# Counting a graph's adjacency matrix with one-hot products: 25 blocks of 50 target nodes, interleaved with a feed-forward layer

## The reference, cut to what matters

```
x, src, dst                                   # (1250, 512), (20000,), (20000,), sorted by dst
...
neigh_sum  = segment_sum(x[src], dst, 1250)   # for each target node: the sum over its edges
neigh_mean = neigh_sum / maximum(deg, 1)[:, None]
h_neigh    = neigh_mean @ W_neigh.T
...
# mixer, its feed-forward part
y = y + gelu(ln(y) @ W1 + b1) @ W2 + b2
```

## Time and profile before

| | before |
|---|---|
| median of 3 executions | 1814.36 us (1813.27 to 1814.72) |
| profiled execution: its span | 1813.0 us, the profile gives no time of its own beside the span |
| TensorE busy with products | 1575.6 us, 87% of the span |
| VectorE, ScalarE, GpSimd busy | 680.0, 368.5, 447.3 us |
| mean granted TensorE clock | 0.937 of full speed |

### The profile page before, as it was taken

The page is one execution under the profiler, slowest core; times in us unless marked ns, Lnnn a source line. Parts: engine busy times, 40 slices in busy tenths (PEclk is TensorE's granted clock), DMA queues, the critical chain, the costliest instruction groups (busy, mean ns, idle before and its releaser), DMA issues.

```text
span 1813.0 us, 18937 instructions
## 1 busy us (share of the span) xinstructions
PE 1575.6 (87%) x7450; PEld 1028.1 (57%) x7450; DVE 680.0 (38%) x1202; ACT 368.5 (20%) x606; POOL 447.3 (25%) x421
## 2 busy tenths in 40 slices
PE   5999969899997957979999989899899746998994
PEld 3537544356554746757777744555768534654551
DVE  4131160599602471436666525330433551111100
ACT  2300011011301022334444411100224201110010
POOL 4000030110111030138888846000210104222112
PEclk9999989989999978989999999999999857999997
DMA  6000100100220002120110042000200762999993
GB/s 185 0 0 1 48 1 0 64 1 0 76 63 0 0 6 105 44 59 22 29 37 22 9 124 46 0 23 0 93 1 1 303 221 88 402 405 401 420 419 101
DMA packets 24004, 173.24 MB, mean 96 GB/s; under 512 B 4520, under 2 KB 5066, under 8 KB 17659
## 3 DMA queue, kind: packets, MB, share of 16 engines
q1 hardware_dynamic: 20028, 166.66, 24.9%
q0 software_dynamic: 3584, 5.12, 1.3%
q10 hardware_dynamic: 313, 0.35, 0.1%
HBM read 153.06 MB, written 16.49 MB: 94 GB/s over the span
## 4 chain that ended last, share of the span: by engine, by line
PE 73%; DVE 9%; DMA 8%; issue 3%; POOL 2%; ACT 2%; SPq 1%; DVEq 0%; POOLq 0%; ACTq 0%
PE psum L896 17%; PE psum L905 8%; PE psum L927 7%; PE psum L1039 6%; PE psum L1339 6%; PE psum L1135 5%; DMA out_x<-arena,idx 4%; PE psum L919 4%; PE psum L1321 3%; PE psum L1123 3%; PE psum L1094 3%; PE psum L1124 2%; PE psum L1261 2%; DMA arena<-in_w_down 2%; DVE ln_st L1358 1%
## 5 line engine op out<-in xcount | busy, mean ns | idle before, releaser
L896 PE MATMUL psum<-arena 125*128 125x512 f32 (+3 forms) x864 | 308.3, 519 | 3.3 <-ACT arena L753 1.4
L896 PEld LDWEIGHTS psum<-arena 125*128 125x128 f32 (+1 forms) x864 | 164.7, 191 | 146.3 <-issue 144.3
L609 POOL TENSOR_TENSOR arena<-arena 125x420 f32<-125x420 f32 x192 | 178.5, 930 | 27.2 <-ACT arena L821 1.0
L1339 PE MATMUL psum<-arena 128*39 128x512 f32 (+1 forms) x704 | 158.2, 606 | 13.2 <-DMA arena<-in_w_down 8.7
L1575 DVE TENSOR_REDUCE neg_max<-psum 125x1 fp32r<-125x1250 f32 x80 | 116.8, 1459 | 113.0 <-PE psum L1094 113.0
L927 PE MATMUL psum<-arena 128*125 128x512 f32 (+3 forms) x424 | 143.5, 498 | 11.1 <-issue 3.9
L821 ACT ACTIVATE arena<-psum 125x420 f32<-125x420 f32 x240 | 107.8, 521 | 130.5 <-PE psum L1124 130.5
L1039 PE MATMUL psum<-arena 125*125 125x512 bf16 (+1 forms) x588 | 119.9, 358 | 13.0 <-DVE arena L1490 11.5
L927 PEld LDWEIGHTS psum<-arena 128*125 128x125 f32 (+2 forms) x424 | 73.9, 190 | 77.9 <-issue 66.2
L1339 PEld LDWEIGHTS psum<-arena 128*39 128x39 f32 (+1 forms) x704 | 51.2, 117 | 114.3 <-issue 109.7
L1489 DVE TENSOR_SCALAR arena<-arena,src_f 125x1250 bf16<-125x1250 f16 x196 | 112.1, 572 | 7.8 <-issue 6.8
(11 more groups left out here) (301 smaller groups left out, 2027.4 us busy)
## 6 DMA issues: line engine op xcount, KB each, us to landing
arena<-in_w_down SPq DMA_DIRECT2D x32, 2816.0 KB, 23.4
arena<-in_w_up SPq DMA_DIRECT2D x32, 682.5 KB, 19.4
a_spill<-arena SPq DMA_DIRECT2D x1, 5468.8 KB
arena<-a_spill SPq DMA_DIRECT2D x1, 5468.8 KB
bc<-k_dram SPq DMA_DIRECT2D x16, 312.5 KB, 4.6
gw<-in_gw SPq DMA_DIRECT2D x2, 2048.0 KB, 10.4
arena<-in_wkqv SPq DMA_DIRECT2D x1, 3072.0 KB, 19.6
k_dram<-arena SPq DMA_DIRECT2D x1, 2500.0 KB, 7.3
```

Of the source, the lines that this page charges most:

```text
L609: pool.tensor_tensor(SUMS[rnd % 2], SUMS[rnd % 2], PT[s % P_RING], ALU.add).then_inc(sum_added, 1)
L896: ins = pe.matmul(o[0:w, lo:hi], lhs(c, m), rhs(c)[:, lo:hi], start=c == 0, stop=c == k - 1)
L1339: ins = pe.matmul(o[64 * j:64 * j + CAP, :], ACTT[g % 2][0:w, f, at:at + CAP], DN[e % 5][0:w, f], start=f == 0, stop=f == FT - 1)
```

## The change

Counts become 25 blocks ("windows") of 50 target nodes. For one edge tile there is one product: the stationary operand `row_hot` is the one-hot of the source's row inside its node tile (125 columns, and a 126th column of ones, which makes the degree), the moving operand `win_hot` is the one-hot of a key of 500 columns, (source's node tile) x 50 + (target inside the window). The result, 126 partitions by 10 node tiles by 50 targets, has sources on partitions, as `agg0` wants it, so nothing is turned; ScalarE drains each window once into `ADJ` (`drain_window`). A window takes at least two bodies of four edge tiles: the first body is written out straight with buffers of its own, the others run in a loop.

The windows no longer follow `w2`. Windows 0 to 11 are placed after the twelve column pieces of `w1`, the other 13 after the ten tiles of `w2`. `w2` moves to the `col_psum` ring, and the windows have the `row_psum` ring. VectorE makes the keys (33 comparisons of 125x160 among them) beside projection `k`, the windows' loop bounds beside `q`, and the one-hots one window ahead of TensorE. The degree is summed by VectorE from the drained row of ones (30x1250 out of 30x12500) and turned by ten small products after `agg0`. GpSimd's additions of `sage_be` to X still wait until `w2` is drained. Several tiles change their slots, and the loads of `wm2`, `ws` and `wn` their places in the queue.

```diff
-            col_stage("w1", 4, lambda c, m: WM1[:, c, ch(m)], lambda c: HT[:, c], C)
+            pe.wait_ge(range_ready, 1)
+            loops_from = [1]
+            def window(w):
+                if w >= 2:
+                    pe.wait_ge(win_free, w - 1)
+                o = row_psum(w)
+                loops_to = pe.value_load(ranges[0:1, w:w + 1], min_val=2)
+                for s in range(BODY):
+                    pe.wait_ge(first_ready, BODY * w + s + 1)
+                    pe.matmul(o[0:TOK + 1, 0:WIN_COLS], row_hot[s], win_hot[s], start=s == 0, stop=False,
+                              skip_group_check=True).then_inc(first_free, 1)
+                with pe.Fori(loops_from[0], loops_to) as i:
+                    for s in range(BODY):
+                        pe.wait_ge(hot_ready[s], i)
+                        pe.matmul(o[0:TOK + 1, 0:WIN_COLS], row_hot[BODY + s], win_hot[BODY + s], start=False, stop=False,
+                                  skip_group_check=True).then_inc(hot_free[s], 1)
+                loops_from[0] = loops_to
+                pe.matmul(o[0:1, 504:505], ones_bf[:], ones_bf[:], start=False, stop=True,
+                          skip_group_check=True).then_inc(win_full, 1)
+            for m in range(4):
+                o = open_col(COL["w1"] + m)
+                for j, (lo, hi) in enumerate(CHUNKS):
+                    for c in range(C):
+                        ins = pe.matmul(o[:, lo:hi], WM1[:, c, ch(m)], HT[:, c, lo:hi], start=c == 0, stop=c == C - 1)
+                    if j == 2:
+                        ins.then_inc(cols_full, 1)
+                    window(3 * m + j)
...
-            row_stage("w2", TILES, lambda c, t: GT[:, c, tok(t)], lambda c, t: WM2[:, c], C)
+            for t in range(TILES):
+                o = open_col(COL["w2"] + t)
+                for c in range(C):
+                    ins = pe.matmul(o[0:TOK, 0:D], GT[:, c, tok(t)], WM2[:, c], start=c == 0, stop=c == C - 1)
                 ins.then_inc(cols_full, 1)
+                for w in windows_after(t):
+                    window(w)
...
             col_stage("agg0", 4, lambda t, m: XN[:, t, ch(m)], lambda t: ADJ[:, t], TILES)
+            pe.wait_ge(deg_row_ready, 1)
+            o = open_row(ROW["deg"])
+            for t in range(TILES):
+                ins = pe.matmul(o[0:TOK, t:t + 1], deg_row[:, tok(t)], ident[96:TOK + 1, TOK:TOK + 1], start=True, stop=True)
+            ins.then_inc(rows_full, 1)
...
+            def one_hots(w):
+                loops_to = dve.value_load(ranges[0:1, w:w + 1], min_val=2)
+                shift = dve.value_load(ranges[0:1, WINDOWS + w:WINDOWS + w + 1])
+                def one_hot(s, tile, ready):
+                    dve.tensor_scalar(win_hot[s], win_iota, float(WIN_COLS * w), edge_key[:, bass.ds(tile, 1)],
+                                      ALU.add, ALU.is_equal)
+                    dve.tensor_scalar(row_hot[s][:, 0:TOK], win_iota[:, 0:TOK], edge_row[:, bass.ds(tile, 1)], None,
+                                      ALU.is_equal).then_inc(ready, 1)
+                for s in range(BODY):
+                    if w:
+                        dve.wait_ge(first_free, BODY * (w - 1) + s + 1)
+                    one_hot(s, loops_from[0] * BODY + shift + (s - BODY), first_ready)
+                with dve.Fori(loops_from[0], loops_to) as i:
+                    for s in range(BODY):
+                        dve.wait_ge(hot_free[s], i)
+                        one_hot(BODY + s, i * BODY + shift + s, hot_ready[s])
+                loops_from[0] = loops_to
+            for w in range(WINDOWS_W1 + 1):
+                one_hots(w)
...
+                for w in windows_after(t):
+                    if w + 1 < WINDOWS:
+                        one_hots(w + 1)
+                dve.wait_ge(cols_full, COL["w2"] + t + 1)
+                o = col_psum(COL["w2"] + t)
+                dve.tensor_tensor(X[:, t], o[0:TOK, 0:D], X[:, t], ALU.add).then_inc(cols_free, 1)
```

More of the change, by code:

```diff
@@ L101, in adds_done, with windows_after @@
     return ADDS * rnd + max(1, t)
[L104 to L108, removed]
+def windows_after(t):
+    first = WINDOWS_W1 + sum(WINDOWS_W2[:t])
+    return range(first, first + WINDOWS_W2[t])
 LN_ORDER = [(n, g) for n in ("mix1", "mix2") for g in range(3)]
@@ L244, in build, with counts @@
-        H = rows(6, at=C * N + C * D)
+        WM1, WM2 = mat(6, 0, C, D), mat(6, C * D, C, D)
+        A_LAST = TILES * N - 2 * SLOT
+        def counts(slot, lo, hi):
+            return arena[lo:hi, slot * SLOT:slot * SLOT + TILES * N].rearrange("p (t n) -> p t n", n=N)
+        ADJ, ADJ_DEG = counts(3, 0, TOK), counts(3, 96, TOK + 1)
+        ADJ_OUT = counts(3, 0, TOK + 1)
+        ADJ1 = counts(6, 0, TOK)
+        win_iota = part(5, A_LAST + 4, WIN_COLS // 2, TOK).bitcast(F16)
+        win_hot = [part(5, A_LAST + 4 + 250 + 250 * s, 250, TOK).bitcast(BF16) for s in range(2 * BODY)]
@@ new lines, in build @@
+        row_hot = [part(5, A_LAST + 4 + 2250 + 64 * s, 64, TOK).bitcast(BF16)[:, 0:TOK + 1] for s in range(2 * BODY)]
+        deg_row = k_sq[96:TOK + 1, :]
+        src_f, dst_f = part(2, 0, EDGE_TILES, EDGE_TILE), part(2, 160, EDGE_TILES, EDGE_TILE)
+        src_tile, dst_win = part(2, 320, EDGE_TILES, EDGE_TILE), part(2, 480, EDGE_TILES, EDGE_TILE)
+        below, touched, marks, up_t, down_t = [part(2, 640 + 160 * i, EDGE_TILES, WINDOWS) for i in range(5)]
+        bodies, body_lt = part(2, 1440, EDGE_TILES // BODY, WINDOWS), part(2, 1480, EDGE_TILES // BODY, WINDOWS)
@@ new lines, in _, with count_steps @@
+            dve.wait_ge(loads["edges"], 32)
+            done(dve.tensor_copy(part(2, 0, 2 * EDGE_TILES, EDGE_TILE), edge_i))
+            def count_steps(total, values, step, n):
+                done(dve.tensor_scalar(total, values, float(step), None, ALU.is_ge))
+                for k in range(2, n):
+                    done(dve.scalar_tensor_tensor(total, values, float(step * k), total, ALU.is_ge, ALU.add))
+            count_steps(src_tile, src_f, TOK, TILES)
+            dve.scalar_tensor_tensor(edge_row[:], src_tile, -float(TOK), src_f, ALU.mult, ALU.add)
@@ L1437, in _ @@
+            done(dve.tensor_scalar(rng[:, 4], rng[:, 3], 1.0, None, ALU.add))
+            dve.tensor_copy(ranges[:], rng[:, 4:6].rearrange("p k w -> p (k w)")).then_inc(range_ready, 1)
             dve.wait_ge(loads["bv"], 16)
```

264 lines of the change are left out of this document (120 added, 144 removed).

## The result

The changed kernel takes 1756.68 us (median of 4 runs, 1755.47 to 1759.5), the kernel before, measured beside it, 1814.15 us (1813.27 to 1814.72). The ratio is 0.9676, with an interval from 0.9661 to 0.9692: 57.5 us faster, where 91.5 us were forecast. 1756.7 us lies outside the range of 1707 to 1744 us.

The account below looks back on a forecast made before the run. The counts, 148 us of a 1813.0 us span, were taken as the bound, with TensorE leading after the change. Savings of 88.5 + 3.0 = 91.5 us gave a span of 1721.5, plus 1.4 a median of 1722.9 us; range 1707 to 1744.

Parts of the forecast that it names:

- What bounds, the number of products: Counts hold the path for 148 us; 200 products of 500 columns replace three for each of 196 edge tiles.
- TensorE's sum: From `w1` to `agg0`: 2.38 us a window, 132.6 us in all, so `agg0` starts 88.5 us earlier.
- Better than that: Rival: loop costs hidden altogether on TensorE, 1.8 us a window, 14.5 us less, 1708 us; chance 0.08.
- VectorE's sum: One-hots at 0.5 us a pair, 4.6 us a window, stay below TensorE's time, in `w2` by only 3 us.
- VectorE leads: Rival: register instructions and waits make a one-hot pair 0.6 to 0.65 us, total 1729 to 1738 us; chance 0.18.
- The wait of 3.35 us before `v`: TensorE's wait for the bounds' chain goes; less 0.3 us for added products, 3.0 us saved.
- Beside `k`: About 37 key operations on VectorE, 11.5 to some 20 us, in an idle of 18.35 us: nothing.
- beside `q`: 14 smaller VectorE operations, under 5 us in an idle of 15.32 us: nothing.
- after `w2`: GpSimd's additions and splits and the degree's reduction (14.6 us) hidden beside `agg0`, turned products in a later wait: nothing.
- Windows with a third body: Rival that the change doesn't do what it says; the counted inputs were said to exclude it.
- one element a cycle: Rival: VectorE's wide comparison takes about 0.65 us, a pair 0.82, total 1778 up to 1795 us; chance 0.06.
- GpSimd against VectorE: Rival: GpSimd blocks VectorE's fast comparisons, 2.7 us a pair, losing over 300 us; chance of slower 0.02.

Follow-up runs that it names:

- fixed tiles: Changed kernel with one-hots reading edge tiles at fixed places, not by register index: 1719.56 us with loops and loads kept, 1713.49 us without them.
- the doses: Changed kernel with the check ahead of the narrow comparison only, the wide one only, or two more assertions a pair: 1741.66, 1746.99 and 1812.43 us.
- the windows behind `w2`: Changed kernel with all 25 windows run one behind the other after `w2`, checks kept: 1833.62 us, ratio 1.0097 to the kernel before.

## Why the prediction was wrong

*What bounds, the number of products.* Right: 200 products (100 in straight bodies, 100 in loops), and the stretch is what moved.

*TensorE's sum.* The product was right: four take 351.11 − 350.26 = 0.85 us, 0.21 each. Its 0.36 us for closing a window and 0.3 us for load and loop were 1.78 − 8 x 0.21 = 0.1 us together; the loops cost TensorE nothing in the open, since fixed tiles with and without them take the same 121.5 us. The whole stretch is 120.5 us when TensorE leads, not 132.6: 12 us too high; the rival *Better than that* had the right price, 1.8 us a window, for TensorE. The two errors had opposite signs: VectorE put the stretch 41 us above TensorE's own sum, and the forecast missed by 29 only because that sum was too high.

*VectorE's sum.* This is the step that failed. "I take 0.5 us a pair and 0.6 us a window for loads and loop" should have been 0.63 and 1.4 us. The 0.26 + 0.17 us of the engine were exact, the wide comparison's two steps cost nothing. But "0.056 us each, so the issuing alone needs about 0.4 us" is 7 x 0.056 and so prices all seven instructions of a pair alike (the five register instructions alone would give 0.28); the doses give 0.07 us for each of the five and 0.28 us for the two comparisons together: 5 x 0.07 + 0.28 = 0.63. From 0.43 us for the engine and 0.4 for the sequencer the prediction then took 0.5 as a margin above both, which was not enough. That VectorE would lead "from 0.54 us a pair on" was borne out as far as runs stand: it leads at 0.55 and 0.57 us and mostly does not at 0.43; where between them the point lies is open. The rival *VectorE leads* named the mechanism and a pair of 0.6 to 0.65 us, with a chance of 0.18, and still came out at 1729 to 1738 us, for it kept 0.6 us for a change of window. With the queue empty that change is in the open: 1.06 us more than a pair's step from window to window, 0.17 us at the loop's entry, and in every other window 0.37 us inside a body. The ten additions, 6.9 us in the prediction, cost next to nothing beside that. 199 x 0.63 + 25 x 1.4 = 160 us on VectorE, 161.9 measured for the stretch.

*The other edits.* The wait of 3.35 us before `v` is gone (0.38 us is left). Yet `w1` starts only 0.27 us earlier. In this profile `k` begins at a granted clock of 0.72 from 28 to 34 us and takes 35.36 us. Of the eleven profiled kernels with the new front, seven show that and start `w1` at 267.2 to 268.0 us; four show 1.00 there, take 33.81 us for `k`, and start it at 263.98 to 265.65, 2.1 to 3.8 us before 267.75. So the saving is there against the one profile of the kernel before, which has 1.00, and seven of eleven executions give most or all of it back. The front is the same program in all eleven; what decides between them is open. *Beside `k`*, *beside `q`* and *after `w2`* cost nothing, as said: the degree's reduction took 23.6 us instead of 14.6 and GpSimd's splits ended at 466.8 us, both inside `agg0`.

*The other rivals.* Windows with a third body, one element a cycle, and GpSimd against VectorE did not occur; the last is real where the additions meet the one-hots, as the windows behind `w2` showed, but here they don't.

## What to carry to other kernels

An engine that runs short instructions has two rates, that of its datapath and that of its sequencer; sum both from the program, every register instruction and the operations themselves, and take the larger. Before indexing an operand by a computed register, make its range provable or check it once for a group: here eight checks in place of one for each body of four tiles cost 41 us of 1757. A cost that a queue hides (loads, branches) is hidden only while the sequencer is ahead, so the same change of window was worth nothing measurable in one version and 1.4 us, 35 us in all, in the other.

## What the runs showed of the hardware

VectorE's sequencer: about 0.07 us for each register instruction or assertion alike and 0.28 us for the two comparisons of a pair (pairs of 0.55 to 0.57, 0.63 and 0.91 us with four, five and nine of them); it runs at least eight instructions ahead of the engine (13 pairs 0.42 us apart behind GpSimd's additions). A comparison of float16 with bfloat16 out keeps its rate with a second arithmetic step, 500 elements in 0.27 us from start to start, where 0.26 was worked out from the one-step form. A reduction of 30 x 12500 float32 elements with a stride took 23.6 us, 1.9 ns an element, where an addition of 1250 takes 1.17 ns each.
